# Half-precision in- and down projections in the second layer of a two-layer network, with squares, head norm and row splits on GpSimd and new order tables

## The reference

```
zxbcdt = x @ in_proj_w.T                     # 256 -> 512 (z) + 768 (xBC) + 8 (dt)
xBC = silu(conv4(xBC) + conv_b); dt = softplus(dt + dt_bias)
S = exp(dt*A)*S + (xs*dt) B^T ; y = S C + D*xs          # scan over tokens
y = y*silu(z); y = y*rsqrt(mean(y*y) + 1e-5)*norm_w; x + x + y @ out_proj_w.T
...                                                     # mLSTM, parallel form:
C = (q k^T / 8) * exp(log_D - max_log_D); h = (C / normalizer) v
h = (h - mean(h)) * rsqrt(var(h) + eps) * scale         # per head of 64
...                                                     # feed-forward, 256 -> 1024 -> 256:
h = gelu(x @ (alpha1*sign(w1)).T + b1); out = h @ (alpha2*sign(w2)).T + b2
```

## Time and profile before

| what | us |
|---|---|
| median of 3 runs | 1158.86 (1156.52 to 1159.09) |
| the profiled execution: its time, and its span | 1157.71, 1156.0 |
| PE busy, DVE busy in the span | 1109.2 (96%), 824.5 (71%) |
| ACT busy, POOL busy in the span | 671.1 (58%), 324.6 (28%) |

### The profile page before, as it was taken

One profiled execution on the slowest core, in us unless ns is written; L12 is line 12 of the kernel. 1 busy time (PEld: TensorE's weight loads), 2 busy tenths in 40 slices (PEclk: granted clock), 3 DMA queues, 4 the chain that ended last, 5 costly groups with the idle time before them and its releaser, 6 DMA issues.

```text
span 1156.0 us, 23649 instructions
## 1 busy us (share of the span) xinstructions
PE 1109.2 (96%) x8692; PEld 922.6 (80%) x8692; DVE 824.5 (71%) x2589; ACT 671.1 (58%) x1423; POOL 324.6 (28%) x354
## 2 busy tenths in 40 slices
PE   7999999999999999999999999989999999999996
PEld 6778888768888877888867888868788887888875
DVE  5825558884668783668883767898797877887673
ACT  4237555236665436656425765586558866678573
POOL 5699956990037100026300003302000001000000
PEclk9999999999999999999999999998999989999999
DMA  8200000100000100000100201210000101000000
GB/s 335 113 19 1 2 1 1 56 20 1 2 1 2 55 20 1 2 2 2 37 20 5 73 1 46 69 51 1 2 19 2 47 1 29 19 2 28 28 20 19
DMA packets 21393, 33.33 MB, mean 29 GB/s; under 512 B 11424, under 2 KB 12192, under 8 KB 20128
## 3 DMA queue, kind: packets, MB, share of 16 engines
q1 hardware_dynamic: 21280, 31.82, 8.1%
HBM read 27.62 MB, written 4.19 MB: 28 GB/s over the span
## 4 chain that ended last, share of the span: by engine, by line
PE 80%; DVE 11%; ACT 6%; issue 2%; POOL 0%; DMA 0%; DVEq 0%; SPq 0%; ACTq 0%
PE ps L498 48%; PE ps L654 4%; PE ps L672 2%; PE ps L671 2%; PE ps L646 2%; DVE z L1631 2%; PE ps L644 2%; PE ps L670 2%; PE ps L914 2%; PE ps L513 1%; PE ps L610 1%; PE ps L701 1%; PE ps L874 1%; DVE pq L1475 1%; PE ps L623 1%
## 5 line engine op out<-in xcount | busy, mean ns | idle before, releaser
L498 PE MATMUL ps<-wts,arena 128*128 128x256 f32 (+2 forms) x1008 | 196.0, 350 | 4.8 <-ACT arena L1392 2.7
L2150 POOL TENSOR_TENSOR pq<-pq 128x512 f16<-128x512 f32 x72 | 83.9, 1166 | 406.0 <-ACT pq L1239 406.0
L498 PE MATMUL ps<-arena,wts 128*128 128x256 f16 (+1 forms) x1344 | 184.6, 290 | 8.6 <-DVE arena L1445 6.3
L498 PEld LDWEIGHTS ps<-wts,arena 128*128 128x128 f32 (+1 forms) x1008 | 149.8, 151 | 40.1 <-ACT arena L1392 3.2
L498 PEld LDWEIGHTS ps<-arena,wts 128*128 128x128 f16 (+1 forms) x1344 | 149.6, 113 | 30.4 <-DVE arena L1445 6.7
L1631 DVE SCALAR_TENSOR_TENSOR z<-ps,small,z 128x256 f32<-128x256 f32 x256 | 123.9, 484 | 22.9 <-PE ps L498 6.0
L1516 DVE CUSTOM_DVE_ANT_0 pq<-ps,mb 128x128 f32<-128x128 f32 x128 | 36.9, 288 | 106.2 <-PE ps L646 105.6
L498 PE MATMUL ps<-wts,pq 128*128 128x256 f16 x864 | 106.4, 273 | 4.5 <-DVE z L1631 1.7
L2198 POOL TENSOR_TENSOR z<-z,wts 128x512 f32<-128x512 f32 x8 | 10.3, 1282 | 318.3 <-PE ps L513 318.3
L498 PEld LDWEIGHTS ps<-wts,pq 128*128 128x128 f16 x864 | 83.4, 98 | 17.8 <-POOL pq L2150 3.4
L1236 ACT ACTIVATE pq<-ps 128x512 f32<-128x512 f32 x72 | 42.8, 595 | 83.8 <-PE ps L498 83.3
(11 more groups left out here) (290 smaller groups left out, 2488.9 us busy)
## 6 DMA issues: line engine op xcount, KB each, us to landing
cT<-in_cT SPq DMA_DIRECT2D x16, 256.0 KB, 2.7
wts<-in_up SPq DMA_DIRECT2D x1, 2304.0 KB, 18.4
wts<-in_down SPq DMA_DIRECT2D x1, 2304.0 KB, 23.8
xT<-in_xT SPq DMA_DIRECT2D x8, 256.0 KB, 4.1
xin<-in_x SPq DMA_DIRECT2D x8, 256.0 KB, 2.9
xmid<-xin SPq DMA_DIRECT2D x8, 256.0 KB, 2.0
wts<-in_w SPq DMA_DIRECT2D x2, 1024.0 KB, 4.9
wts<-in_c SPq DMA_DIRECT2D x16, 128.0 KB, 3.1
```

What stands on the lines that cost most here:

```text
L498: ins = mm(out_, l, r, start=(n == 0), stop=(n == len(pairs) - 1))
L2150: G.tensor_tensor(lo, abuf(s, e), hi, ALU.subtract).then_inc(*po.up(("alo", s, e)))
```

## The change

Layer 1 changes in these ways, all in one edit:

- The in-projection goes in float16. GpSimd scales its weights by 16 and splits them into a high and a low half, in the last turn of layer 0 (`split_in`, before that turn's `lows`). ACT writes the input's high half and a new DVE instruction (`lower`) its low half. Each float32 product becomes three float16 ones. The scaling is taken back in the convolution's weights, in silu's scale and in `dt_in`.
- The down projection goes in float16. Gelu's result goes to a buffer `gl` (four slots that all units share), an added ACT copy makes the high half in float16, GpSimd the low half, and two products with the bare signs replace each float32 one. `alpha2` is multiplied in afterwards by an added DVE instruction in `ffn_out`.
- GpSimd adds the squares, so that two of the eight matmuls of `rms` are left. It does the four instructions of the heads' norm, the five of the split in `rows`, and the last three of the five in `csrow`.
- All five tables are written anew. Over the whole of layer 1 ACT issues 50 table loads where it issued 58.

```diff
@@ the order tables (all five are written anew; two lines of one)
-    1.load.1 0.load.0 0.load.1 1.load.0 0.ztc.0 2.load.1 0.ztc.1 1.ztc.0 3.load.1 2.load.0 1.ztc.1 3.load.0
+    0.csrow.0 1.load.0 0.load.0 0.csrow.1 0.sq.0 0.sq.1 0.rows.0 0.load.1 1.csrow.0 1.csrow.1 0.rows.1 2.load.1
+    1.sq.0 0.heads.0 1.sq.1 2.load.0 1.load.1 0.heads.1 2.csrow.0 0.up.0.4 0.ztc.0 0.up.0.0 0.up.0.6 0.up.0.2
...
@@ -447,2 +462,4 @@
+        rests = (rest[:, :], t1e[0:8, 0, :])
         def zbuf(g, s):
@@ -878,3 +895,13 @@
+def inproj(s, key, m0, m, ring):
+    eng.wait_ge(*pe.at("winh"))
+    eng.wait_ge(*pe.at("zTa", s, "out"))
+    o = take((key, s, m), (key, s, m, "out"), spot(RINGS[ring]))
+    for j in range(2):
+        ins = group(o[:, j * T:j * T + T],
+                    [(winh[k][:, m0 + m + j, a_, :], xh[s][:, b_, k, :]) for k in range(KC) for a_, b_ in THREE])
+    ins.then_inc(*pe.up((key, s, m)))
 def mamba_dt(s):
+    eng.wait_ge(*pe.at("winh"))
     eng.wait_ge(*pe.at("zTa", s, "out"))
@@ -883,3 +910,4 @@
         ins = group(o[:, t * MH:t * MH + MH],
-                    [(xT[s][:, k, t * P:t * P + P], win[:, k, 2 * DI + 2 * DS:]) for k in range(KC)])
+                    [(xh[s][:, b_, k, t * P:t * P + P], wdth[k][:, a_, :])
+                     for k in range(KC) for a_, b_ in THREE])
     ins.then_inc(*pe.up(("dt", s)))
@@ -921,7 +949,6 @@
     ysq = carve_m(s)[4]
-    for m in range(0, DM, 2):
-        eng.wait_ge(*pe.at("ysq", s, m))
+    eng.wait_ge(*pe.at("yss", s))
     o = take(("ss", s), ("ss", s, "out"))
     for t in range(TT):
-        ins = group(o[:, t:t + 1], [(ysq[:, m, t * P:t * P + P], onesq[:, 0:1]) for m in range(DM)])
+        ins = mm(o[:, t:t + 1], ysq[:, 0, t * P:t * P + P], onesq[:, 0:1], start=True, stop=True)
     ins.then_inc(*pe.up(("ss", s)))
@@ -980,2 +1007,11 @@
+def ffn_down(s):
+    for m in range(0, FM, 2):
+        eng.wait_ge(*pe.at("hl", s, m))
+    o = take(("f2", s), ("f2", s, "out"), spot(RINGS["b"]))
+    for t in range(TT):
+        ins = group(o[:, t * C:t * C + C], [(hTh(s)[:, i, m, t * P:t * P + P], w2h[:, m, :])
+                                            for m in range(FM) for i in range(2)])
+    ins.then_inc(*pe.up(("f2", s)))
 def sign_turns(d, cc, r0):
@@ -1012,6 +1048,6 @@
         s, m = n
-        colproj(s, "xbc", win[:, :, DI:2 * DI + 2 * DS], xT[s], [("zTa", s, "out")], m, m + 2, "c")
+        inproj(s, "xbc", DM, m, "c")
     if step == "zg":
         s, m = n
-        colproj(s, "zg", win[:, :, 0:DI], xT[s], [("zTa", s, "out")], m, m + 2, "b")
+        inproj(s, "zg", 0, m, "b")
     if step == "dsum":
@@ -1080,3 +1116,3 @@
                 eng.wait_ge(*pe.reached((None, "wT", 1, cc, 0, "out")))
-        rowproj(s, "f2", w2T, hTb(s), [("f1", s, m, "out") for m in range(0, FM, 2)], spot(RINGS["b"]), kc=FM)
+        ffn_down(s)
 pe.turn = None
@@ -1253,3 +1289,3 @@
         for s in range(NS):
-            evict(("zTa", s), flat(xT[s]))
+            evict(("zTa", s), xh[s][:, 0].rearrange("p k t -> p (k t)"), outmark=("zTah", s))
         act.turn = g
@@ -1344,3 +1380,3 @@
         eng.wait_ge(*act.at("zg", s, m))
-        A(flat(carve_m(s)[1][:, m:m + 2, :]), psv(("zg", s, m)), ACT.Silu).then_inc(
+        A(flat(carve_m(s)[1][:, m:m + 2, :]), psv(("zg", s, m)), ACT.Silu, scale=1.0 / UPS).then_inc(
             *act.up(("zg", s, m, "out")))
@@ -1390,6 +1426,10 @@
         eng.wait_ge(*act.at("f1", s, m))
+        if (turn, s) > (TURNS, 0):
+            eng.wait_ge(*act.reached(((turn, "hl", 0, m) if s else (turn - 1, "hl", NS - 1, m))))
         for j in range(2):
-            A(hTb(s)[:, m + j, :], psv(("f1", s, m))[:, j * T:j * T + T], ACT.Gelu,
+            A(gl[:, m // 2, j * T:j * T + T], psv(("f1", s, m))[:, j * T:j * T + T], ACT.Gelu,
               scale=al1[:, m + j:m + j + 1], bias=b1[:, m + j:m + j + 1]).then_inc(
                 *act.up(("f1", s, m, "out") if j else None))
+        eng.wait_ge(*act.own())
+        A(flat(hTh(s)[:, 0, m:m + 2, :]), gl[:, m // 2, :], ACT.Copy).then_inc(*act.up(("hh", s, m)))
     if step == "ln6":
@@ -1741,2 +1781,4 @@
                     eng.wait_ge(*v.at("halfo" if g else "halfk"))
+                    if g == TURNS - 1:
+                        eng.wait_ge(*v.at("winh"))
                     residual(1, "xo", z[1][:, :, :], z2[1], "ln_2")
@@ -1780,4 +1822,3 @@
     eng.wait_ge(*v.at("wT", 1, cc, 0))
-    V_.tensor_tensor(w2T[:, cc, :], psv(("wT", 1, cc, 0))[:, 0:C], al2r, ALU.mult).then_inc(
-        *v.up(("wT", 1, cc, 0, "out")))
+    V_.tensor_copy(w2h[:, cc, :], psv(("wT", 1, cc, 0))[:, 0:C]).then_inc(*v.up(("wT", 1, cc, 0, "out")))
@@ -1800,5 +1841,4 @@
     eng.wait_ge(*v.at("dt", s))
-    V_.tensor_tensor(th(sm(s, 0), MH), th(psv(("dt", s))[:, 0:2 * MH], MH), rowb(dtb, MH),
-                     ALU.add).then_inc(
-        *v.up(("dt", s, "out")))
+    V_.scalar_tensor_tensor(th(sm(s, 0), MH), th(psv(("dt", s))[:, 0:2 * MH], MH), 1.0 / UPS,
+                            rowb(dtb, MH), ALU.mult, ALU.add).then_inc(*v.up(("dt", s, "out")))
     v.mark(("dtx", s, "x"))
@@ -1834,17 +1874,8 @@
-def parts(c3_, src, n, marks):
-    V_.tensor_copy(c3_[0:n, :], src).then_inc(*v.up())
-    eng.wait_ge(*v.own())
-    V_.tensor_tensor(rest[0:n, :], src, c3_[0:n, :], ALU.subtract).then_inc(*v.up(marks[0]))
-    eng.wait_ge(*v.own())
-    V_.tensor_copy(rest1[0:n, :], rest[0:n, :]).then_inc(*v.up())
-    eng.wait_ge(*v.own())
-    V_.tensor_copy(c3_[32:32 + n, :], rest1[0:n, :]).then_inc(*v.up())
-    V_.tensor_tensor(c3_[64:64 + n, :], rest[0:n, :], rest1[0:n, :], ALU.subtract).then_inc(
-        *v.up(marks[1]))
 def mamba_rows(s):
+    src = psv(("csr", s))[0:MH, 0:T]
     eng.wait_ge(*v.at("csr", s))
-    parts(c3[s], psv(("csr", s))[0:MH, 0:T], MH, [("csr", s, "out"), ("csr3", s)])
+    V_.tensor_copy(c3[s][0:MH, :], src).then_inc(*v.up())
+    eng.wait_ge(*v.own())
+    V_.tensor_tensor(rests[s], src, c3[s][0:MH, :], ALU.subtract).then_inc(*v.up(("csr", s, "out")))
@@ -1970,14 +1999,3 @@
 def mlstm_h2(s):
-    x = flat(z2[s][:, :, :])
-    x8 = x.rearrange("p (h d) -> p h d", h=TT * LH)
-    eng.wait_ge(*v.at("ln_h", s, "rstd"))
-    V_.tensor_tensor(x8, x8, mv[s][:, :, 0:1].to_broadcast([P, TT * LH, LD]), ALU.subtract).then_inc(*v.up())
-    eng.wait_ge(*v.own())
-    V_.tensor_tensor(x8, x8, rstd[s][:, :].unsqueeze(2).to_broadcast([P, TT * LH, LD]),
-                     ALU.mult).then_inc(*v.up())
-    eng.wait_ge(*v.own())
-    V_.tensor_tensor(z2[s][:, :, :], z2[s][:, :, :], rowb(onorm, C), ALU.mult).then_inc(*v.up())
-    eng.wait_ge(*v.own())
-    V_.tensor_tensor(z2[s][:, :, :], z2[s][:, :, :], zbuf(v.turn, s)[:, :, :], ALU.add).then_inc(*v.up())
-    eng.wait_ge(*v.own())
+    eng.wait_ge(*v.at("hd", s))
     ln_stats(s, "ln_5", z2[s])
@@ -1991,6 +2009,9 @@
 def ffn_out(s):
-    eng.wait_ge(*v.at("z5b", s))
+    y = hTb(s)[:, 0:TT * C]
     eng.wait_ge(*v.at("f2", s))
-    V_.tensor_tensor(z2[s][:, :, :], psv(("f2", s)).rearrange("p (t c) -> p t c", t=TT), z2[s][:, :, :],
-                     ALU.add).then_inc(*v.up(("f2", s, "out")))
+    V_.tensor_tensor(y.rearrange("p (t c) -> p t c", t=TT), psv(("f2", s)).rearrange("p (t c) -> p t c", t=TT),
+                     rowb(al2r, C), ALU.mult).then_inc(*v.up(("f2", s, "out")))
+    eng.wait_ge(*v.at("z5b", s))
+    eng.wait_ge(*v.own())
+    V_.tensor_tensor(flat(z2[s][:, :, :]), y, flat(z2[s][:, :, :]), ALU.add).then_inc(*v.up())
     eng.wait_ge(*v.own())
@@ -2003,2 +2024,4 @@
     s = n[0] if n else None
+    if step == "load":
+        lower(("zTa", n[0]), ("zTah", n[0]), xh[n[0]], ("zTa", n[0], "out"))
     if step == "al":
@@ -2182,3 +2205,28 @@
 po.stage("low")
+def split_in():
+    eng.wait_ge(*po.at("p2weights"))
+    G.tensor_scalar(flat(ck), flat(ck), 1.0 / UPS, None, ALU.mult).then_inc(*po.up())
+    for k in range(KC):
+        for c, n in [(c, min(512, WIN - c)) for c in range(0, WIN, 512)] + [(WIN, MH)]:
+            w = win[:, k, c:c + n]
+            G.tensor_scalar(w, w, UPS, None, ALU.mult).then_inc(*po.up())
+            eng.wait_ge(*po.own())
+            G.tensor_copy(half1[:, 0, 0:n], w).then_inc(*po.up())
+            eng.wait_ge(*po.own())
+            G.tensor_tensor(half1[:, 1, 0:n], w, half1[:, 0, 0:n], ALU.subtract).then_inc(*po.up())
+            eng.wait_ge(*po.own())
+            for i in range(2):
+                if n == MH:
+                    G.tensor_copy(wdth[k][:, i, :], half1[:, i, 0:n]).then_inc(*po.up())
+                else:
+                    G.tensor_copy(winh[k][:, c // P:(c + n) // P, i, :],
+                                  half1[:, i, 0:n].rearrange("p (n e) -> p n e", e=P)).then_inc(*po.up())
+            eng.wait_ge(*po.own())
+    po.turn = None
+    po.mark("winh")
 for g in range(1, TURNS):
+    if g == TURNS - 1:
+        split_in()
     po.turn = g
@@ -2187,2 +2235,11 @@
 po.stage("layer1")
+def thirds(c3_, r, n, mark):
+    G.tensor_copy(rest1[0:n, :], r).then_inc(*po.up())
```

(47 more changed lines are left out.)

192 lines of the change are left out of this document (102 added, 90 removed).

## The result

| | us, median | ratio to before, 95% interval |
|---|---|---|
| before (5 runs) | 1158.25 (1156.52 to 1159.09) | |
| after (5 runs) | 1151.68 (1151.32 to 1153.69) | 0.9947 (0.9933 to 0.9961) |
| forecast | 1125 (1104 to 1148) | |

The change makes the kernel faster, by 6.6 us, a fifth of what was forecast. The time lies outside the range.

What follows compares the result with a forecast made beforehand. The prediction took PE's work to set the time: 1157.7 - 57.6 (work) + 20.2 (idle time) + 1.4 (start) + 3.2 (tail) = 1124.9, forecast as 1125 us, range 1104 to 1148.

Steps and rivals of the forecast that it cites:

- PE's work: Layer 1's cheaper `in`, `zg`, `down` and `rms` take 57.6 us off PE, leaving 334; nothing taken for `dt`.
- The clock: PE's granted clock in layer 1: no change taken; bounds half of today's 16 us gained, as much again lost.
- The recorded sign: The prediction counts as wrong if layer 1's granted PE clock leaves 0.92 to 0.98.
- PE's idle time: PE's 19.8 us without work in layer 1 taken as doubling to 40, adding 20.2 us.
- The port's 1145: Rival: DVE and POOL obstruct each other in layer 1, DVE at 325 us, PE idle 60; 1144.7 us, chance 0.13.
- DVE: Layer 1 busy time 303 us: 287 after net work, plus 16 of excess beside GpSimd (bounds 0 to 38).
- ACT: Layer 1 busy time 289 us: 20 us of gelu copies added, 10 us of table loads gone.
- POOL: Layer 1 busy time 150 us: 128 of new work beside the present 22.6.
- The weight split: GpSimd's split in layer 0's last turn, 28 us, done at about 678 with 13 us margin; no cost taken.
- Start: Layer 1's first `in` step waits for DVE's last norm and two `lower` instructions: 1.4 us more.
- Tail: The last unit's chain at the kernel's end gets 3.2 us longer, with nothing to hide it.
- The slower rival: The chain through POOL sets layer 1's time, 50 us plus 20 of queueing exposed; 1170 us, chance 0.08.

Runs made afterwards that it cites:

- pe_light: The kernel after with 8 float16 matmuls instead of 12 in in- and gate projections, 16 instead of 32 in down projections; 1143.0 us, ratio 0.9891.
- square of code and order: Before and after plus two mixed kernels: before with after's five tables, 1203.8 us; after with four of before's tables, 1205.0 us.
- fill_pauses: The kernel after with 134 extra matmuls, results overwritten, ahead of waits where PE stands still for 2 us or more; 1145.9 us, ratio 0.9896.
- pool_light: The kernel after with GpSimd's squares, heads' norm and gelu low halves (from the second turn) cut to 16 columns; 1135.0 us, ratio 0.9820.

## Why the prediction was wrong

The direction was right, and PE's work fell as the rows said. What failed is the step from there to the time: "what PE has to do sets the time", so each us off PE comes off the sum, with a guess for the idle time and nothing for the clock. In pe_light 31 us less of PE's work brought 6.5. In the sum two terms failed.

- **PE's work**, -57.6: measured 58.1 at the full clock. `in` and `down` hit their rows; `dt` saved 0.5 us a step where I took nothing. With these 4 us the parts add up to 62, so the agreement of the total is partly luck.
- **The clock**, "I take no change; the bounds are half of today's 16 us gained and as much again lost": it is 20.6 us more, beyond the upper bound. I had read in the earlier trace rows that it falls with PE busy on narrow matmuls, and did not ask what pauses do, though the sum itself put twice the idle time into the stage. That is the larger failure: between before and after the growth stands behind PE's pauses. Filling them took 14.4 us of it back, 9.5 more than the same matmuls did behind the waits. The recorded sign, a clock outside 0.92 to 0.98, came true with 0.89.
- **PE's idle time**, "I take twice that, 40", with start and tail 24.8 more than before: measured 33.0 more. It was a guess by analogy, from the idle time of another order. The square of code and order shows that this does not carry over: the same old code has 20 us of it under one order and 41 under the other.
- These two and the work close the gap: 1124.9 + 20.6 + 8.2 - 0.5 = 1153.2, the profiled execution's time. The 20.6 is no price: fill_pauses, with 14.4 of it back, gained 5.9. No rival had it. The port's 1145 came nearest, by 60 us of idle time (52.8 came) and not for its reason.
- **DVE**: 313 for my 303. The net work went as taken (287 would be left), the excess beside GpSimd is 26 us, within 0 to 38, and not 16. The small instructions have 16 us of it (last section). pool_light's DVE falls by 17 us with 64 us of GpSimd's work.
- **ACT** 285 (289 taken), **POOL** 150.0 (150), table loads 50: right.
- **The weight split**, nothing, done by 678: done by 672, right.
- **Start**, 1.4: the first product with the mask begins 2.3 us later. **Tail**, 3.2: from the last unit's head statistics to the end 33.9 us and 30.1 before, 3.8.
- **The slower rival**, GpSimd's chain exposed by 70 us: not in that size. POOL has 1% of the chain of waits. Making its new work nearly free in pool_light brought 15 us, nearly all in the stretch where the clock is 0.81 in after and 1.00 there.

What stays open: what an order fitted anew to this code, with PE's pauses priced, would give. The stretches of half clock without a pause are not explained either. Those that were looked at, and 1043 to 1060, hold narrow matmuls; no run took these away.

## What to carry to other kernels

When the busiest engine loses a seventh of its work and the order is written anew, don't take its idle time from the old trace. Price the saved work at well under 1 when the second engine is within a fifth of the first: here 31 us off PE alone brought 0.2 us for each, on this order. Read the granted clock beside the busy time, and look for PE's pauses of 2 us with a long run at half clock behind them. Extra matmuls ahead of the wait are a cheap test of what such a pause costs, and the same matmuls behind the wait tell the pause from the matmuls.

## What the runs showed of the hardware

The contention of VectorE with GpSimd reaches the smallest instructions, which I had not counted. DVE after, and GpSimd at the same time:

```profile
1100.76 0.17 DVE L1978 SCALAR_TENSOR_TENSOR small<-wts 128x4 f32<-128x4 f32 x1 [4.02 <-ACT wts L1139]
1102.27 0.82 DVE L1978 SCALAR_TENSOR_TENSOR small<-wts 128x4 f32<-128x4 f32 x1 [1.34 <-ACT wts L1139]
1103.12 1.19 DVE L1980 TENSOR_TENSOR small<-small 128x8 f32<-128x8 f32 x1
...
1116.12 0.17 DVE L1980 TENSOR_TENSOR small<-small 128x8 f32<-128x8 f32 x1
```

```profile
1099.65 3.41 POOL L2264 TENSOR_TENSOR arena<-wts,arena 128x512 f16<-128x512 f32 x3
1103.02 1.26 POOL L2298 TENSOR_TENSOR z<-z,wts 128x512 f32<-128x512 f32 x1
```

An instruction of 4 or 8 columns takes 0.17 us with GpSimd idle (1116.12); the one of 1100.76 met the seam between GpSimd's first low half and its second. The one from 1102.27 ends at 1103.09, as GpSimd's third low half does (1103.06), and the next ends at 1104.31, as GpSimd's next instruction does (1104.28). So they end when GpSimd's instruction ends. That agrees with the rule of the Trainium skill, SBUF — State Buffer, section on the two separate sides, which the prediction weighed for large instructions alone: the loser of the shared ports waits out the whole instruction. The three large groups above account for 10 of the 26 us of excess (32 x 0.127, 16 x 0.148, 24 x 0.156). The instructions on `small` with up to 16 columns, 208 in both kernels, went from 35.0 to 51.1 us, which is the other 16.

pool_light shows that GpSimd is the cause, as it changes nothing on VectorE. With GpSimd's instructions short, these groups are back at their durations of before (946, 692, 405 and 161 ns) or half the way to them:

```profile
L1901 DVE TENSOR_TENSOR pq<-pq,wts 128x768 f32<-128x768 f32 x32 | 30.3, 953 | 1.1 <-ACT pq L1315 0.9
L1913 DVE TENSOR_TENSOR arena<-arena 128x512 f32<-128x512 f32 x16 | 12.3, 767 | 1.7
L1469 DVE TENSOR_SCALAR z<-z,wts 128x256 f32<-128x256 f32 x24 | 9.5, 438 | 1.5 <-ACT wts L1135 1.5
L1978 DVE SCALAR_TENSOR_TENSOR small<-wts 128x4 f32<-128x4 f32 x16 | 2.3, 161 | 10.8 <-ACT wts L1139 10.0 <-ACT small L1408 0.7
```

The last took 375 ns on average in after.
